# A fused early-fusion transformer on one core: another order of the token streams' 310 steps

## What is computed

```python
h = concat([patch_embedding(x), text_embedding(x_txt)], axis=1)
h = h + latent_attention(layernorm(h))   # 12 heads of 16, softmax, values normalised per head
h = h + dense_mixture(layernorm(h))      # 5 experts of width 256, all of them run, top 2 weighted
h = h + causal_attention(layernorm(h))   # 6 heads of 32
h = h + sparse_mixture(layernorm(h))     # 8 experts of width 512, top 2, limited capacity
return h
```

## Time and profile before

| | |
|---|---|
| median of three runs | 4488.57 us |
| the runs | 4482.95 to 4501.21 us |
| span of the profiled execution | 4603.4 us |
| PE busy over the span | 4185.6 us, 91% |
| DVE busy | 2891.6 us, 63% |
| ACT busy | 2281.9 us, 50% |
| POOL busy | 2372.9 us, 52% |

### The profile page before, as it was taken

The page is one execution under the profiler, slowest core; times in us unless marked ns, Lnnn a source line. Parts: engine busy times, 40 slices in busy tenths (PEclk is TensorE's granted clock), DMA queues, the critical chain, the costliest instruction groups (busy, mean ns, idle before and its releaser), DMA issues. The chain is left out here.

```text
span 4603.4 us, 78782 instructions
## 1 busy us (share of the span) xinstructions
PE 4185.6 (91%) x27140; PEld 3385.6 (74%) x27140; DVE 2891.6 (63%) x8103; ACT 2281.9 (50%) x5250; POOL 2372.9 (52%) x2435
## 2 busy tenths in 40 slices
PE   3899999999999999999999999999997699999999
PEld 2567777776777676777777776767676599999999
DVE  4477777777777777777777777776764333333333
ACT  1455565555555555555555555555553233333333
POOL 2355555555555555555555555555554155555555
PEclk7799999999999999999999999999998699999999
DMA  8500000000000000000000000000000122222220
GB/s 160 95 10 12 12 9 12 9 12 11 11 13 11 11 10 15 12 12 9 12 9 12 10 11 11 11 11 11 13 9 26 42 47 47 72 69 53 70 51 19
DMA packets 159100, 122.25 MB, mean 27 GB/s; under 512 B 63839, under 2 KB 150454, under 8 KB 158710
## 3 DMA queue, kind: packets, MB, share of 16 engines
q1 hardware_dynamic: 124086, 80.29, 7.8%
q0 software_dynamic: 34624, 36.92, 3.1%
HBM read 76.84 MB, written 74.58 MB: 33 GB/s over the span
## 5 line engine op out<-in xcount | busy, mean ns | idle before, releaser
L866 ACT ACTIVATE probs<-bank_a 128x384 f32<-128x384 f32 (+2 forms) x1728 | 692.5, 453 | 668.7 <-PE bank_a L967 436.7
L1220 DVE TENSOR_REDUCE neg_max<-bank_v 128x1 f32<-128x352 f32 (+3 forms) x1728 | 778.0, 492 | 245.2 <-PE bank_v L942 128.3
L745 POOL TENSOR_SCALAR hidden<-hidden 128x384 f32<-128x384 f32 x320 | 386.8, 1209 | 777.1 <-ACT hidden L887 775.7
L942 PE MATMUL bank_v<-heads_t 50*128 50x352 f32 (+4 forms) x1728 | 407.2, 405 | 119.1 <-DVE neg_max L1220 69.6
L985 PE MATMUL bank_o<-probs,v 128*32 128x384 f32 (+3 forms) x3456 | 455.3, 492 | 4.0 <-issue 2.6
L942 PEld LDWEIGHTS bank_v<-heads_t 50*128 50x128 f32 (+1 forms) x1728 | 210.6, 194 | 334.9 <-DVE neg_max L1220 141.2
L1533 POOL DMA_INDIRECT out_tokens<-res,token x232 | 233.0, 1005 | 372.4 <-DVE res L1718 321.2
L967 PE MATMUL bank_a<-heads_t 50*128 50x384 f32 (+3 forms) x1728 | 391.5, 392 | 30.4 <-ACT probs L866 26.2
L1104 PE MATMUL bank_a<-ffn_x,w_ffn 128*128 128x384 f32 x1600 | 390.6, 377 | 0.0
L1113 PE MATMUL bank_v<-w_down,hidden 128*128 128x192 f32 x1920 | 355.2, 335 | 5.8 <-DVE hidden L1380 4.2
L707 POOL TENSOR_TENSOR rstd<-ve,pow_half 128x3 f32<-128x3 f32 x128 | 113.0, 883 | 474.1 <-DVE ve L1156 473.8
(11 more groups left out here) (246 smaller groups left out, 9308.8 us busy)
## 6 DMA issues: line engine op xcount, KB each, us to landing
xs_dram<-zeros SPq DMA_DIRECT2D x29, 780.0 KB, 18.4
rows<-xs_dram SPq DMA_DIRECT2D x232, 96.0 KB
out_tokens<-h_z SPq DMA_DIRECT2D x32, 288.0 KB, 2.3
rows<-xs_dram SPq DMA_DIRECT2D x232, 33.5 KB
hidden<-in_w SPq DMA_DIRECT2D x8, 512.0 KB
hidden<-in_w SPq DMA_DIRECT2D x16, 256.0 KB
sofar<-out_tokens,token POOLq DMA_INDIRECT x232
out_tokens<-res,token POOLq DMA_INDIRECT x232
```

Of the source, the lines that this page charges most:

```text
L745: step(pool.tensor_scalar(gate_tanh[:, m, :], gate_tanh[:, m, :], 1.0, None, ALU.add))
L866: act.activation(probs[:, n % NPROBS, i, lo:T], empty("score", k, g, kt, i)[:, lo:T], ACT.Exp, scale=DHS[k] ** -0.5).then_inc(a_free, 1)
L942: mm = pe.matmul(bank[:, 0:keys], heads_t[k][r:r + rows, b, tile[t]], heads_t[k][r:r + rows, 6 + b, 0:keys], start=True, stop=(k == 0))
L1220: dve.tensor_reduce(neg_max[k][g % 2][:, t, at:at + 1], bank[:, 0:keys], AX.X, ALU.max, negate=True).then_inc(v_free, 1)
```

## The change

Only the string changes. The four streams' lists, the instructions of each step, the buffers and their number, and the string for a last single round are as before.

```diff
-ORDER = ("wzzyzzzzyzyxyzzyzxxzxxzyxzxxzxyzyxyzxzzyyyzzzzxzxzzyxzxzyzzzxzxyzzzxzyzxzzzxzzxxzxxyxxzx"
...
+ORDER = ("zzyzzzzyzyxzzyzyxxzxxzyzxzyzzxzzxxyyzzzzyzyzxzzxzzzwzxxzyzxzyxzzxyxzxxzzzxzxzyyxxzzxxwxzxyx"
...
```

More of the change, by code:

```diff
@@ L55 @@
                 "zxxzxxyxxxzxzxyzxxxxyxxwxxxxzxxyxxxzzxxyxxxwzyxzxxxxzyywyxxxxxxxxxx")
-ORDER = ("wzzyzzzzyzyxyzzyzxxzxxzyxzxxzxyzyxyzxzzyyyzzzzxzxzzyxzxzyzzzxzxyzzzxzyzxzzzxzzxxzxxyxxzx"
-         "zxzzxxxyxxyzxxzxxzxxyzxxxxzyxxzxxxzxxyzxzxxyxwwxxxxyyxxzyzzxxxzxxwxxzxzyzzzyyxzzyzyxxzxx"
-         "zzyzxxzxzxyzyxyzzzxzzxzzzyyzzzzzxwxzzyzxzxzwxzxwzzxyzxzzxxzxxyxxzxzxzzxxwxyxxyzxxzxxzxxy"
-         "xxxzxzyxxzxxxzxxyxzxxzyyxyzzxxxxyxxxyxyxxyxxxx")
+ORDER = ("zzyzzzzyzyxzyzzyxxzxxzyzxzyzzxzzxxyyzzzzyzyzxzzxzzzwzxxzyzxzyxzzxyxzxzzzxzxzyyxxzzxxwxzxyx"
+         "xzzxxxzwyxxyxxxxzyxxzzxxxxyxxzyxxwxyxxyzxxxyzxzzwxxxyxzzxxzxxxzxxxxzxzyzzyzyxyzzyzxxzyxzzx"
+         "xyzyyxzxzxyzzzzyxzxyzzzxzzzxzzxzyzxyzyzxzzxyxzzxzzxzzxxzxxzxxyxzxzzxxxyxxzxxxxyxxzwxxxxzxx"
+         "yzxxxzyxxzyxxxwzzxwyzxxxxyzyzxxxxxxxyxxx")
 STREAM_OF_NORM = (0, 2, 2, 3)
```

## The result

The changed kernel took 4611.73 us (median of 4 runs, 4602.53 to 4631.15), against 4494.89 for the kernel before: a ratio of 1.026, with a 95% interval of 1.0229 to 1.0291. It is **slower by 117 us**. The forecast was 4527, slower by 0.85%, and the measured time lies above the stated range of 4430 to 4590: the sign was right and the size was not.

A forecast was written before the change was run, and what follows sets the result against it. PE, busy 93% of the steady part, was taken as the bound. Terms 3.3 + 2.5 + 2.0 - 1.8 - 3.4 = +2.6 us a pair, 39 us in fifteen, gave 4527 us (0.85% slower), range 4430 to 4590.

The forecast's parts named there:

- the clock: PE's granted clock over the whole kernel: the forecast sum included no loss from stretches at half clock.
- the middle: Matmuls moved from both round ends go among the maxima and cover DVE's short holes: -3.4 us a pair, other bound 0.
- What bounds it: Steady part: PE, busy 93%, is a queue of matmuls with short holes; order can change only holes and clock.
- The values in round A: PE's hole before the "up" half of `ffn 1 1`, behind `values 2` waiting for POOL's power: +3.3 us a pair.
- Round B: The values in round B: the hole at PE's first blocked maxima grows from 0.79 to about 3.3 us, +2.5 a pair.
- the rival of a shorter power: POOL's power is shorter than its 6.16 us row, both values holes go: -4.6 us a pair, 4422 us; chance 0.12.
- The end of round A: From the third shift on, filler matmuls leave ACT's fixed chain and part comes back as holes: +2.0 us a pair.
- The end of round B: The 3.08 us hole before `sums` shrinks, as POOL's power of `stats 2` comes ahead of six DMAs: -1.8 a pair.
- the fronts of the rounds: Swapped steps at the front of each round, costed at nothing with `rows` and the carry.
- the rival named 1.7 us for each hole: Slower, with the clock: half clock follows both forecast values holes; 6.8 us a pair, 4588 us; chance 0.12.
- Given back: Other engines catch up during the values holes, later holes shrink: half back 4484 us, chance 0.24; whole 4442, chance 0.18.

The follow-up runs named there:

- `val_early`: The new order with `values 1` and the blocks step ahead of it taken forward in both rounds; 4542.6 us, ratio 1.010 to the kernel before.
- `before_val_close`: The kernel before with only `values 1` of round A moved later, four steps instead of eleven ahead of `values 2`; 4608.4 us, ratio 1.0242.
- the control: The kernel before, unchanged, run and profiled again together with the experiments; 4485.3 us, 210.4 us a pair of rounds.
- `before_split`: The kernel before with the six DMAs of `places` split in round B, the last ones issued behind POOL's power of `stats 2`; 4472.7 us, ratio 0.9935.
- `half_B_before`: Round A in the new order, round B in the order of before; 4643.9 us, ratio 1.033 to the kernel before.
- `val_busy`: `val_early` with every score matmul of the last group of stream x's attention in round A issued twice; 4558.5 us, ratio 1.014 to the kernel before.

## Why the prediction was right or wrong

Two terms of the sum failed: the clock, which it put at nothing and which was half of the loss, and the middle. The others came near, though not always for the reason given.

**What bounds it: right.** PE's work stayed at 189 to 192 us a pair in all these orders.

**The values in round A: right in mechanism, too large.** +3.3 was forecast, 2.75 - 0.58 = +2.2 came, at the matmuls that were named. The three passes of `values 2` took 1.05 + 0.76 + 0.76 us instead of 0.75 + 1.59 + 0.94 as in the order before, so the bank came free 0.7 us earlier. **Round B: the same**, +2.5 forecast, 2.70 - 0.79 = +1.9 came. That the two together cost about 1.5%, all that follows from them included, is shown by `val_early`, that the distance alone can cost over 2% by `before_val_close`. That the power holds DVE for its 6.15 us is shown by DVE's wait of 3.72; the rival of a shorter power is out.

**The end of round A: +2.0 forecast, +1.9 came as holes** (1.00 ahead of `down 3`, 1.06, 0.39, 0.73 and 0.61 to the end of the round, against 0.73, 0.57 and 0.61 in the control). That its half clock would cost more than its holes wasn't seen.

**The end of round B: -1.8 forecast, about -1.7 came**, but at another place. The difference that was named, the power behind the six DMAs, was the cause (`before_split`), but of the hole of 2.44 ahead of `xt 2`, which is gone, and not of the late copy ahead of `sums`; 0.73 at the last scores is new. That the figures agree is partly luck.

**The middle, -3.4: this step failed.** By the total, 3.8 less the four terms' 2.2 + 1.9 + 1.9 - 1.7 = 4.3, it brought -0.5, together with the fronts of the rounds, which were put at nothing. The hole ahead of `xt 0` went from there, -1.4; so the middle by itself made the holes 0.9 us a pair longer. The 3.4 was also badly made up: it takes 0.58 out of three rows of DVE's, though the profile gives that hole to ACT. DVE's waits did shrink: without the values' holes, the three rows under L942 that name DVE come to 52 us in the control (40.4 + 11.6 + 10.8 - 14 x 0.79) and to 19 now (48.7 + 8.4 - 14 x 2.70), 2.3 us a pair. But ACT is late now: its waits at L967 behind the exponentials rose by 43.5 us, 3.1 a pair, half of them outside the end of round A (0.73 of that at the end of round B), another 0.8 a pair came behind its copies at L845, and small holes grew at half a dozen other lines. That the moved blocks are what makes ACT late is likely by their place, but no run shows it by itself. I looked only at the engine that was late, not at the one that would be.

**The clock: the step that cost most.** The sum took no clock loss at all, and the rival named 1.7 us for each hole longer than 3.08. It was +4.1 us a pair, half of the result. Neither hole reached 3.08, and yet the one of 2.75 was followed by 6.9 us at half clock and the one of 2.68 by none. The Trainium skill, "TensorE: Matmul & The Clock Gate", section "Why this matters for your kernels", has idle gaps between bursts of matmuls bring the half rate back. The holes of 2.75 us in the new order and of 5.45 us agree; the same hole of 2.75 in `half_B_before`, followed by no half clock in five of twelve pairs, and the one of 2.68 don't. The stretches at 1242.5 and at the end of round A follow no single long hole, and the repeated matmuls of `val_busy` didn't prevent the latter, so by these runs the rule covers a part of the loss. **What starts the others stays open.** The base hid the term: the execution profiled before had 10.1 us of clock loss a pair, so the trace looked as if half clock were there in any order, while the control had 4.8.

**Given back: wrong.** Little of the values' holes came back later. `val_early` took 2.75 and 1.60 us out of them, 4.35 a pair; all holes together fell by 3.8, and the pair by 3.4.

## What to carry to other kernels

When an order of steps is rearranged, price the distance between a slow helper's input and the wait for its result, in time of the waiting engine's other work: here 6.15 us on GpSimd, hidden in one order, cost about 69 us in the other, by `val_early`. Moving the consumer later doesn't help when all that follows needs it; move the producer earlier. And when the busiest engine has few holes (here 7% of its time), look at the clock row beside the holes, and check that the profiled execution is an ordinary one before the sum is made against it.

## What the runs showed that was not expected

DVE's passes depend on what POOL does beside them. `values 2`'s second pass takes 1.52 us in the control, with POOL's elementwise steps alongside all the time, and 0.76 in the new order. By form, 28 times in the control and 27 in the new order:

```profile
L1208 DVE TENSOR_TENSOR v<-v,lng 128x576 f32<-128x576 f32 x28 | 42.7, 1525 | 1.0
```

```profile
L1208 DVE TENSOR_TENSOR v<-v,lng 128x576 f32<-128x576 f32 x27 | 20.5, 758 | 0.9
```

In round A of the new order POOL has just ended the power and issues `rows`. But in round B the pass takes 0.76 as well, although POOL's L747 runs beside it, and there L747 is slow, 1.50 us instead of 1.00, and so is DVE's third pass, 1.43 instead of 0.76:

```profile
1377.29 0.76 DVE L1208 TENSOR_TENSOR v<-v,lng 128x576 f32<-128x576 f32 x1
1378.08 1.43 DVE L1211 TENSOR_TENSOR v<-v,lnb 128x576 f32<-128x576 f32 x1
```

```profile
1377.39 1.50 POOL L747 TENSOR_TENSOR hidden<-hidden 128x384 f32<-128x384 f32 x1
```

The Trainium skill's "GPSIMD Engine Reference", section "Specifications", says that GpSimd shares its SBUF interfaces with VectorE and contends with its instructions of two SBUF inputs. These passes have two, and the traces agree that the two engines slow each other; which of them gives way in which pass stays open.

The half clock repeats exactly in some orders and not in others. In the new order eleven of twelve pairs of rounds have the same three stretches of the same length at the same steps, in the control they come and go from pair to pair (its pairs take 207.9 to 212.4 us). The two profiled executions of the kernel before differ by 5 us a pair, and the clock loss accounts for it.
